# Router logits as extra columns, tokens scattered to expert slots, and weight splits moved to GpSimd, in a two-layer transformer with experts

## The reference, cut to what matters

```python
# one expert per sequence, by argmax of cond_8: 256 -> 512 -> 256
up = x @ wu.T + bu;  gate = x @ wg.T + bg
x2 = (silu(up) * gate) @ wd.T + bd
# router and capacity: 2048 tokens, 8 experts, top 2, 640 slots per expert
logits = x2 @ Wg.T
top_v, top_i = top_k(logits, 2);  gates = softmax(top_v)
pos = cumsum(onehot(flat_e), axis=0) - 1, taken at the expert of each pair
keep = pos < cap
exp_batches = zeros(E, cap, d).at[flat_e, min(pos, cap)].set(x[tok], mode='drop')
h = exp_batches @ W1;  inp, g = split(h)
exp_out = (gelu(inp) * g) @ W2
out = segment_sum(where(keep, gates, 0) * exp_out[flat_e, ...], tok)
```

## Time and profile before

| | |
|---|---|
| median of 3 runs | 1047.15 us (1046.93 to 1047.98) |
| the profiled execution | 1051.18 us, span 1049.6 us |
| TensorE busy | 956.4 us, 91% |
| VectorE, ScalarE, GpSimd busy | 519.7, 437.6, 280.4 us |
| chain that ended last | PE 71%, DVE 15%, ACT 6%, issue 5%, DMA 2% |
| mean granted clock of TensorE | 0.967 of 2.4 GHz |

### The profile page before, as it was taken

One profiled execution on the slowest core, in us unless ns is written; L12 is line 12 of the kernel. 1 busy time (PEld: TensorE's weight loads), 2 busy tenths in 40 slices (PEclk: granted clock), 3 DMA queues, 4 the chain that ended last, 5 costly groups with the idle time before them and its releaser, 6 DMA issues.

```text
span 1049.6 us, 13136 instructions
## 1 busy us (share of the span) xinstructions
PE 956.4 (91%) x4864; PEld 795.1 (76%) x4864; DVE 519.7 (50%) x1010; ACT 437.6 (42%) x823; POOL 280.4 (27%) x246
## 2 busy tenths in 40 slices
PE   4899999997849699999669999999999999999898
PEld 3666777786729699999648688888888888887686
DVE  6445344477544754444446743333333333588644
ACT  1454556333114444444323434435334243324775
POOL 8232222102035445453644102304123041000000
PEclk9999999999769999999869999999999999999999
DMA  7010000302032234443152130200302003000011
GB/s 260 1 62 1 1 1 2 131 26 80 31 105 44 86 110 132 131 114 146 36 183 62 28 121 0 103 19 1 121 1 89 32 1 120 1 1 1 1 40 41
DMA packets 19534, 64.57 MB, mean 62 GB/s; under 512 B 3920, under 2 KB 11344, under 8 KB 17040
## 3 DMA queue, kind: packets, MB, share of 16 engines
q1 hardware_dynamic: 14336, 36.72, 9.8%
q0 software_dynamic: 4416, 25.44, 8.2%
q10 hardware_dynamic: 720, 1.58, 0.4%
HBM read 54.30 MB, written 9.44 MB: 61 GB/s over the span
## 4 chain that ended last, share of the span: by engine, by line
PE 71%; DVE 15%; ACT 6%; issue 5%; DMA 2%; POOL 0%; DVEq 0%; ACTq 0%; POOLq 0%
PE banks L853 15%; PE banks L855 14%; PE banks L854 14%; PE banks L1029 4%; PE banks L1027 3%; PE banks L1028 3%; PE banks L923 3%; PE banks L907 3%; PE banks L877 1%; PE banks L1077 1%; PE banks L1076 1%; PE banks L914 1%; PE banks L1063 1%; PE banks L1064 1%; DMA expert_output<-y_rows 1%
## 5 line engine op out<-in xcount | busy, mean ns | idle before, releaser
L853 PE MATMUL banks<-input_hi,mlp_hi 128*128 128x512 f32 x384 | 153.4, 399 | 1.5 <-DVE input_lo L1605 1.5
L855 PE MATMUL banks<-input_hi,mlp_lo 128*128 128x512 f32 x384 | 151.7, 395 | 0.0
L854 PE MATMUL banks<-input_lo,mlp_hi 128*128 128x512 f32 x384 | 150.9, 393 | 0.0
L1812 POOL TENSOR_TENSOR mlp_lo<-weight_stage,mlp_hi 128x768 fp32r<-128x768 f32 x40 | 74.2, 1854 | 239.4 <-ACT mlp_hi L1256 239.4
L1271 ACT CAST hidden_hi<-hidden 128x512 fp32r<-128x512 f32 x96 | 59.5, 620 | 175.5 <-DVE hidden L1615 107.9
L1621 DVE TENSOR_TENSOR hidden_lo<-hidden,hidden_hi 128x512 fp32r<-128x512 f32 x96 | 66.4, 692 | 71.2 <-ACT hidden_hi L1271 71.2
L1615 DVE SCALAR_TENSOR_TENSOR hidden<-banks,L_expert_weight,gelu 128x512 f32<-128x512 f32 x64 | 48.0, 750 | 100.0 <-PE banks L855 94.7
L1782 POOL TENSOR_TENSOR ffn_w_lo<-weight_stage,ffn_w_hi 128x512 fp32r<-128x512 f32 x48 | 62.0, 1295 | 120.2 <-ACT ffn_w_hi L1213 120.2
L853 PE MATMUL banks<-expert_in_hi,ffn_w_hi 128*128 128x320 f32 x256 | 82.7, 323 | 8.4 <-DVE hidden L1569 4.9
L853 PEld LDWEIGHTS banks<-input_hi,mlp_hi 128*128 128x128 f32 x384 | 72.7, 189 | 17.3 <-issue 1.9
L855 PEld LDWEIGHTS banks<-input_hi,mlp_lo 128*128 128x128 f32 x384 | 72.6, 189 | 16.4
(11 more groups left out here) (278 smaller groups left out, 2157.0 us busy)
## 6 DMA issues: line engine op xcount, KB each, us to landing
weight_stage<-in_packF SPq DMA_DIRECT2D x8, 1536.0 KB, 6.9
weight_stage<-in_shared SPq DMA_DIRECT2D x2, 3072.0 KB, 10.5
expert_output<-y_rows SPq DMA_DIRECT2D x40, 128.0 KB
weight_stage<-in_cond_w SPq DMA_DIRECT2D x4, 512.0 KB, 8.1
residual<-in_xT SPq DMA_DIRECT2D x4, 512.0 KB, 14.5
routed_input<-x_rows SPq DMA_DIRECT2D x16, 128.0 KB, 1.7
weight_stage<-in_ffn_w SPq DMA_DIRECT2D x2, 1024.0 KB, 7.8
out_xT<-out SPq DMA_DIRECT2D x8, 256.0 KB, 2.0
```

Of the source, the lines that this page charges most:

```text
L853: pe.matmul(o, wh, dh, start=(i == 0), stop=False)
L854: pe.matmul(o, wh, dl, start=False, stop=False)
L855: last = pe.matmul(o, wl, dh, start=False, stop=(i == len(terms) - 1))
L1812: pool.tensor_tensor(wDl[s][:, qs], stage[:, qs], f(wDh[s][:, qs]), ALU.subtract).then_inc(done)
```

## The change

- **Logits.** The down weights of a sequence get 8 more columns, W_down times the router's weights (`wg`, computed on TensorE from the weights in another layout, `down_by_row`, 1 MB for both sequences), and the bias 8 more values. A down product has 264 columns, and its last 8 are the logits. `xt`, `xcol`, `logit`, `lg` are gone.
- **Scatter.** `digits`, `at`, `inv`, `slots` and the gathers are gone, and SyncE's stores of row tiles. `row` works out each token's row in DRAM; for each tile and choice GpSimd issues one indirect store of 128 rows (`scatter`, 64 in all). A token past the capacity goes to a spare row. SyncE fills the 5120 slots with zeros at the start, and loads an expert's 640 rows with one plain load (`fetch_rows`).
- **Weight splits.** Both sequences' weights are loaded and split in attention(3): `w0_lo` on GpSimd, `w0_hi` on ScalarE as before, and `wg` with `wg_hi` and `wg_lo` behind each. `phase0` keeps the bias loads. Biases are read where they were loaded, without `b0`.
- The rings of banks are 4, 3 and 1 instead of 3, 2 and 2.

```diff
-PK0 = 2 * KD * H0 + (H0 // P) * D + 2 * (H0 // P)
+DG = D + G
+W0N = 2 * KD * H0 + (H0 // P) * DG
+PK0 = W0N + 2 * (H0 // P) + KD
+STAGE_HALF = 3080
 PKF = KD * 2 * I0 + (I0 // P) * D
 PK1 = 2 * KD * I1 + (I1 // P) * D
-W0N = PK0 - 2 * HT
...
     def split0(b):
         for q in range(PIECES0):
             act.append(("w0_hi", b, q))
-            dve.append(("w0_lo", b, q))
-            if q < PIECES0 - 1:
-                yield
-        act.append(("b0", b))
+            pool.append(("w0_lo", b, q))
+            yield
+        dve.append(("b0_wide", b))
+        product("out", "wg", b)
+        act.append(("wg_hi", b))
+        dve.append(("wg_lo", b))
         yield
...
-    pool.append(("ld_pack0", 0))
     share_banks(True)
     run(weave(attention(1), chain(folded(1), rotated("k", 2), rotated("q", 2), value_tiles(2))))
     share_banks(False)
     run(weave(attention(2), chain(rotated("k", 3), rotated("q", 3), value_tiles(3))))
     share_banks(True)
-    run(weave(attention(3), split0(0), 3))
-
-
-    use("work", [(0,), (1,), (2,)])
-    use("down", [(3,), (4,)])
-    use("turn2", [(5,), (6,)])
+    pool.append(("ld_pack0", 0))
+    pool.append(("ld_pack0", 1))
+    run(weave(attention(3), chain(split0(0), split0(1)), 2))
+
+
+    use("work", [(0,), (1,), (2,), (3,)])
+    use("down", [(4,), (5,), (7,)])
+    use("turn2", [(6,)])
 
     def up_chunk(c):
...
+    def route_chunk(c):
+        while c * QT + QT - 1 not in rows_done:
             yield
-        logits(columns)
-        logits_done.add(c)
         yield
-
-    def route_chunk(c):
-        while c not in logits_done:
-            yield
-        for step in ("first", "second", "m16", "first_row"):
+        for step in ("first", "second", "m16"):
             dve.append((step, c))
             yield
+        dve.append(("first_row", c))
         product("turn2", "cnt", c)
+        yield
         dve.append(("pos", c))
         yield
         dve.append(("place", c))
         yield
-        dve.append(("digits", c))
+        dve.append(("row", c))
+        for t in range(QT):
+            for k in range(K):
+                pool.append(("scatter", c, t, k))
         yield
-        for k in range(K):
-            for t in range(QT):
-                dve.append(("at", c, k, t))
-            yield
-            for t in range(QT):
-                if (c, k, t) == (0, 0, 0):
-                    banks["inv", c, k, t] = (7,)
-                pe.append(("inv", c, k, t))
 
     def split_expert(e):
         for k in range(KD):
...
-        weights = chain([None] * 4, split0(1))
+        weights = chain([])
         for c in range(NCH):
             if c == CPB:
                 weights = split_expert(0)
             steps = chain(some(ups[c + 1], HT + 1), down_chunk(c), ups[c + 1]) if c + 1 < NCH else chain([None] * 3, down_chunk(c))
             yield from weave(steps, weights)
 
-    run(weave(weave(all_chunks(), chain(*[chunk_logits(c) for c in range(NCH)])), chain(*[route_chunk(c) for c in range(NCH)])))
-    act.append(("slots",))
+    run(weave(all_chunks(), chain(*[route_chunk(c) for c in range(NCH)])))
...
-                dh, dl = parts(wBh[b], H0)[2], parts(wBl[b], H0)[2]
+                dh, dl = parts(wBh[b], H0, DG)[2], parts(wBl[b], H0, DG)[2]
+                pe.wait_ge(*ready("wg_lo", b))
                 pe.wait_ge(*ready("hid_lo", c, HT - 1))
-                products(o[:, 0:D], [(hidH[n][:, k, ts], hidL[n][:, k, ts], dh[:, k, :], dl[:, k, :]) for k in range(HT)], done)
+                products(o[:, 0:DG], [(hidH[n][:, k, ts], hidL[n][:, k, ts], dh[:, k, :], dl[:, k, :]) for k in range(HT)], done)
...
+            elif kind == "wg":
+                b, = key
                 pe.wait_ge(ld["wg"], 16)
-                for k in range(KD):
-                    last = pe.matmul(o[:, 0:G], xc[:, k, :], wgT[:, k, :], start=(k == 0), stop=(k == KD - 1))
+                pe.wait_ge(ld["by_row"], 16 * B)
+                for k in range(HT):
+                    for m in range(KD):
+                        pe.matmul(o[:, k * G:(k + 1) * G], down_by_row[b][:, m, k * P:(k + 1) * P], wgT[:, m, :], start=(m == 0), stop=(m == KD - 1))
+                pe.wait_ge(*ready("b0_wide", b))
+                for m in range(KD):
+                    last = pe.matmul(o[:, HT * G:(HT + 1) * G], bias_wide[b][:, m, :], wgT[:, m, :], start=(m == 0), stop=(m == KD - 1))
...
+            elif kind == "wg_hi":
...
+                act.wait_ge(*ready("wg", b))
+                act.wait_ge(*ready("w0_lo", b, PIECES0 - 1))
+                act.copy(downB[b][:, D:DG], o[:, HT * G:(HT + 1) * G])
+                act.copy(parts(wBh[b], H0, DG)[2][:, :, D:DG], o[:, 0:HT * G].rearrange("p (k g) -> p k g", g=G)).then_inc(done)
...
-            elif kind == "w0_lo":
-                b, q = key
-                qs = slice(q * W0N // PIECES0, (q + 1) * W0N // PIECES0)
-                dve.wait_ge(*ready("w0_hi", b, q))
-                dve.tensor_tensor(wBl[b][:, qs], stage[:, b * PK0:(b + 1) * PK0][:, qs], f(wBh[b][:, qs]), ALU.subtract).then_inc(done)
+            elif kind == "b0_wide":
+                b, = key
+                col = raw0(b)[:, W0N + 2 * HT:PK0]
+                dve.wait_ge(ld[f"pack0_{b}"], 16)
+                for m in range(KD):
+                    last = dve.tensor_scalar(bias_wide[b][:, m, :], ones32[:, :], col[:, m:m + 1], None, ALU.mult)
+                last.then_inc(done)
+            elif kind == "wg_lo":
+                b, = key
+                dve.wait_ge(*ready("wg_hi", b))
+                dve.tensor_tensor(parts(wBl[b], H0, DG)[2][:, :, D:DG], bank(("wg", b))[:, 0:HT * G].rearrange("p (k g) -> p k g", g=G),
+                                  f(parts(wBh[b], H0, DG)[2][:, :, D:DG]), ALU.subtract).then_inc(done)
...
+                if c >= 2:
+                    dve.wait_ge(st_x[c % NXR], 16 * K * QT * (c // NXR))
...
+                step(dve.tensor_tensor(row[:, :, :], row[:, :, :], all_first_rows[:, c, :, :], ALU.add))
+                dve.tensor_tensor(row_int[c % 2][:, :, :], row[:, :, :], spare[:, c, :, :], ALU.min).then_inc(done)
...
-                pool.wait_ge(*ready("pick0"))
-                pool.wait_ge(*ready("cw"))
-                pool.wait_ge(*ready("half_mask"))
-                pool.indirect_dma_start(stage[:, 0:PK0], None, A["pack0"], bass.IndirectOffsetOnAxis(ap=dyn0[:, 0:1], axis=0)).then_inc(ld["pack0_0"], 16)
+                b, = key
+                if b == 0:
+                    pool.wait_ge(*ready("pick0"))
+                    for b_ in range(B):
+                        pool.indirect_dma_start(stage[:, b_ * KD * H0:(b_ + 1) * KD * H0], None, A["down_by_row"],
+                                                bass.IndirectOffsetOnAxis(ap=dyn0[:, b_:b_ + 1], axis=0)).then_inc(ld["by_row"], 16)
+                    for last in (("kept", "q", NCH - 1), ("v", NCH - 1, QT - 2), ("rope_0", "q", NCH - 1), ("rope_1", "q", NCH - 1),
+                                 ("sines", "q", NCH - 1), ("skip", "q", NCH - 1)):
+                        pool.wait_ge(*ready(*last))
+                    pool.wait_ge(ld["zero"], 16 * G)
+                pool.indirect_dma_start(raw0(b), None, A["pack0"], bass.IndirectOffsetOnAxis(ap=dyn0[:, b:b + 1], axis=0)).then_inc(ld[f"pack0_{b}"], 16)
+            elif kind == "w0_lo":
+                b, q = key
+                qs = slice(q * W0N // PIECES0, (q + 1) * W0N // PIECES0)
+                pool.wait_ge(*ready("w0_hi", b, q))
+                pool.tensor_tensor(wBl[b][:, qs], raw0(b)[:, qs], f(wBh[b][:, qs]), ALU.subtract).then_inc(done)
...
-                pool.indirect_dma_start(got[slot][:, :], None, rows_in, bass.IndirectOffsetOnAxis(ap=slot_token[:, n:n + 1], axis=0)).then_inc(ld[f"gather{slot}"], 16)
...
+            elif kind == "scatter":
+                c, t, k = key
+                pool.wait_ge(*ready("xrow", c, t))
+                pool.wait_ge(*ready("row", c))
+                pool.indirect_dma_start(rows_in, bass.IndirectOffsetOnAxis(ap=row_int[c % 2][:, k, t:t + 1], axis=0), xr[c % NXR][:, t, 0:D], None).then_inc(st_x[c % NXR], 16)
...
+                if n == 0 and q == 0:
+                    pool.wait_ge(*ready("xe", G - 1, ST - 1))
...
+        sp.wait_ge(constants, CONSTS)
+        many = zeros[:, :].rearrange("p (a d) -> p a d", a=1).broadcast_to((P, ST, D))
+        for e in range(G):
+            sp.dma_start(rows_in[e * CAP:(e + 1) * CAP, :].rearrange("(j p) d -> p j d", p=P), many).then_inc(ld["zero"], 16)
...
+        def fetch_rows(e):
+            sp.dma_start(got[e % 2][:, :, :], rows_in[e * CAP:(e + 1) * CAP, :].rearrange("(j p) d -> p j d", p=P)).then_inc(ld[f"rows{e % 2}"], 16)
+
+        for b in range(B):
+            sp.wait_ge(*ready("wg", b))
+        fetch_expert(0)
+        sp.wait_ge(*ready("T", NCH - 1, NH - 1, QT - 1, (TPB - 1) // 4))
+        fetch_expert(1)
+        for c in range(NCH - NXR, NCH):
```

(31 more changed lines are left out.)

192 lines of the change are left out of this document (55 added, 137 removed).

## The result

The changed kernel took 1060.69 us, median of 4 runs (1058.85 to 1061.79); the kernel before took 1047.26 beside it. The ratio is 1.0126, 95% interval 1.0108 to 1.0143: 13.4 us slower, where 3.4 us faster was forecast. The time lies outside the range (1036 to 1053). A repetition gave 1.0115 (1.0098 to 1.0131).

A forecast was written before the change was run, and what follows sets the result against it. TensorE, busy for 91% of the span, was taken to bound the kernel. The terms 5.1 + 7.2 + 2.5 - 15.4 - 0.7 - 2.1 = -3.4 us took 1047.15 to 1043.8 us, range 1036 to 1053.

The forecast's parts named there:

- U: Reference time in the routed layer: the end of the last up product of chunk 3, 275.6 us in the kernel before.
- Part 1: Attention, weight loads: ScalarE's first w0_hi waits for its load, so p_col starts at 159.2 instead of 154.1; +5.1 us.
- Part 2: End of attention: leftover weight-split steps in one block ahead of flush() delay transposes, +7.2 us; half clock after idle TensorE, +2.5.
- the front costs little: Rival at attention: loads land earlier or TensorE has other work, clock stays up; 6.7 us less, 1037; chance 0.20.
- Part 3: Routed layer from the start of the up products behind attention to U: 64.7 us against 80.1, -15.4 us.
- wait 2.2: Routed layer before U: TensorE's wait ahead of chunk 0's count, with one up product run first; 2.2 us.
- 3.3: Routed layer before U: TensorE's wait ahead of chunk 1's count, including one VectorE step blocked by GpSimd's split; 3.3 us.
- the counts stall TensorE more: Rival in the routed layer: both waits for counts reach 4 us and bring half clock; +6, 1050; chance 0.18.
- Part 4: From U to the first expert product: counts, row numbers, sixteen scatters, fetch and tiles take 38.9 us against 39.6; -0.7 us.
- scatters are slower than gathers: Rival on GpSimd's queue from U + 8: at 2.0 us per scatter instead of 1.25, +12, 1056; chance 0.17.
- Part 5: Experts: without gathers, expert 0's wait of 1.27 us and some waits of 0.1 to 0.3 go; -2.1 us.
- At nothing: Items counted as no cost: zero fill of 5.2 MB on SyncE's queue, fetch_rows there, and the mlp split's added wait.

The follow-up runs named there:

- e4: Changed kernel with the two splits of expert 0's down weights moved behind all scatters on ScalarE's and GpSimd's queues: 1057.56 us, 1.0080 to the kernel before.
- e9: Changed kernel with loads, weight splits and counts moved on their queues, and chunk 2's row numbers ahead of chunk 3's row tiles: 1037.32 us, 0.9896 to the kernel before.

## Why the prediction was wrong

Forecast were 3.4 us less, measured 13.4 us more. Two things failed: the counts and row numbers were summed too early (parts 3 and 4), and the last half of the kernel was left out of the sum, though an address changed there.

- **What bounds the kernel** was read rightly: the change decides in front of TensorE, at the end of attention and between U and the experts.
- **Part 1** (+5.1) held: `p_col` stood at 159.59, 5.5 late (forecast 159.2).
- **Part 2** (+7.2, +2.5) came out near its size, in part by luck. Six splits took 7.51 us, as summed. But the block began later than summed: `wg_hi(0)` stood at 185.41 and not at 182.5, since the cast ahead of it was already 7.0 us late (183.28; 176.32 before) and it then waited for TensorE's small products. So the transposes behind `p_col(29)` came 14.4 us late (194.66 against 180.24), where parts 1 and 2 say 12.3. TensorE's idle time was 3.35 us and not over 4, and the half clock cost about 1.5 us instead of 2.5. Together 14.8 were forecast, and `out(3)` came 16.0 late. The rival "the front costs little" is out.
- **Part 3** (-15.4) gave -12.3. The steps that failed are "wait 2.2" and "3.3": they were 2.82 and 3.90. Both are about 0.6 us too short for one reason, which part 4 shares: the sum took from the kernel before that `hid_lo` ends at U + 2.3, and in the changed kernel the first search runs ahead of `prod0`, which makes it U + 3.0 (this is read from the order on VectorE, no edit tried it). The blocked step was rightly sized (1.17 us at 259.19, beside a split on GpSimd). And the half clock, which was only in the upper bound, came behind the second wait (0.76 and 0.89 for 10 us, about 2 us), in some executions behind the first too. With these, 39.9 + 17.6 + 6.7 + 0.7 + 2 = 66.9 of the 67.8. (The bound "-19 (no waits)" is -20.9 by the part's own terms; nothing hung on it.) The rival "the counts stall TensorE more" was the one nearest to the truth here: later counts are worth 7 us.
- **Part 4** (-0.7) gave +4.0. "`hid_lo` ended at U + 2.3, and six steps of 0.22 follow" is the step that failed: it ended at U + 3.0, and one of the six steps took 3.05 us. So the count of the last but one chunk came at U + 7.2 and not at 3.7, its row numbers at U + 11.8 and not at 8.2. The two splits that queued behind chunk 1's eight scatters are 2.9 of these 3.5 us: with them gone (e4) the wait was 4.33. The sum had no split on GpSimd there. Behind it the sixteenth scatter took 1.1 us more than summed; landing, fetch and tiles together were right (11.9 us). (The terms up to "13.0" add up to 12.5; the sixteen scatters decide, not they.) The rival "scatters are slower than gathers" is out: 1.27 us each. The Trainium skill, "SBUF — State Buffer", section "Who interferes with whom", also says that an operation of VectorE with two inputs in SBUF contends with a GpSimd operation that reads SBUF, and that the later one blocks until the first is done. The trace agrees in size (3.05 us against 0.19, with 2.49 on GpSimd), not plainly in the order, since VectorE's record starts 0.5 us ahead; for scatters beside VectorE 1.40 instead of 0.97 us is the most it shows.
- **Part 5** (-2.1) gave -3.9: from the first expert product to the gated experts 217.4 us instead of 221.3.
- **Not in the sum at all**: the last 517 us of the kernel, +4.3 by the trace and 5 to 6 by the runs, from an address.
- **At nothing**: the zero fill holds. That the sum's base mattered was not foreseen either: the trace of before is 4 us above its median.

In sum, by the traces: +1.1 (T0 15.9 late, 14.8 forecast), +3.1, +4.7, -1.8, +4.3 = 11.4 off, and 8.0 instead of -3.4. The other 5.4 us to the medians are differences between executions; why the traced one of before took 4 us more than its median stays open.

## What to carry to other kernels

Before a unit is put on an in-order queue, write down what the queue holds at that moment, leftovers of a weave and bursts of DMA issues among them, and ask for each neighbour who waits behind it; here 23 us lay in queue places (from the changed kernel to e9) and 5 to 6 in an address. Where a burst of issues decides the end, count back from its last one, and let nothing stand ahead of the steps that start it. Compare parts of the trace that no edit touches: if they differ, look at the addresses of their tiles.
